# A four-layer graph network on one core: border steps of the message loop redrawn, and its variance moved to VectorE between two normalising passes

## The reference

```
def layer2(h, adj, W1, b1, g1, be1, W2, b2, g2, be2):
    m_j = einsum('bnd,do->bno', h, W1[:D])
    m_i = einsum('bnd,do->bno', h, W1[D:])
    pre = m_j[:, None, :, :] + m_i[:, :, None, :] + b1      # every pair i, j
    msg = gelu(layernorm(pre) * g1 + be1)                   # exact gelu
    agg = einsum('bijo,bij->bio', msg, adj)
    return layernorm(concatenate([h, agg], -1) @ W2 + b2) * g2 + be2
```

## Time and profile before

| | |
|---|---|
| median of three runs | 4009.07 us |
| profiled execution | 4007.12 us, of which its span 4005.3 us |
| DVE busy | 3267.3 us (82%) |
| PE busy | 3231.7 us (81%), mean granted clock 0.913 |
| ACT busy | 2663.1 us (66%) |
| POOL busy | 1939.6 us (48%) |
| transfers | 41 GB/s read and written over the span |

### The profile page before, as it was taken

How to read it: one execution, slowest core, us unless ns; L and a number is a source line. 1 busy time by engine, 2 the same in 40 slices (tenths; PEclk the granted TensorE clock), 3 DMA queues, 4 the chain that set the end, 5 groups by cost and what they waited for, 6 DMA issues and landing times.

```text
span 4005.3 us, 92223 instructions
## 1 busy us (share of the span) xinstructions
PE 3231.7 (81%) x24743; PEld 2745.1 (69%) x24840; DVE 3267.3 (82%) x11961; ACT 2663.1 (66%) x6659; POOL 1939.6 (48%) x1598
## 2 busy tenths in 40 slices
PE   3484688787888889788788888888897887888888
PEld 2273667677676777767677776767777676776777
DVE  4788888888888888888888888888888888887830
ACT  2484776848667585766848676685857668495753
POOL 1182753719355382744718273461827447182730
PEclk7596889999899999989999998999999899999999
DMA  2010102012020210202011020202102020110200
GB/s 82 29 53 29 50 9 75 24 36 73 5 79 16 67 37 30 72 3 80 24 51 48 30 68 2 83 22 62 37 30 72 4 80 24 41 46 9 61 8 21
DMA packets 147064, 167.74 MB, mean 42 GB/s; under 512 B 13232, under 2 KB 100912, under 8 KB 146736
## 3 DMA queue, kind: packets, MB, share of 16 engines
q1 hardware_dynamic: 146736, 163.96, 13.5%
HBM read 151.33 MB, written 12.58 MB: 41 GB/s over the span
## 4 chain that ended last, share of the span: by engine, by line
issue 27%; PE 20%; POOL 19%; DVE 19%; ACT 9%; DVEq 3%; POOLq 1%; ACTq 0%; DMA 0%; SPq 0%
POOL v_z L570 13%; PE n_bank_c L1604 4%; PE n_bank_d L1621 3%; PE n_bank_d L1622 3%; POOL v_prstd L581 2%; PE n_bank_d L1618 2%; DVE v_top_at L1077 2%; POOL v_pvar L578 2%; PE n_bank_b L1679 2%; ACT v_rows L813 1%; DVE v_top L1074 1%; DVE v_normed L1168 1%; ACT v_pair L878 1%; DVE v_adj_x L1082 1%; PE n_bank_b L1835 1%
## 5 line engine op out<-in xcount | busy, mean ns | idle before, releaser
L570 POOL TENSOR_TENSOR v_z<-v_z,all_bc_L_gnn_be 128x512 f32<-128x512 f32 x620 | 787.1, 1271 | 50.5 <-DVE v_z L1128 24.2
L781 ACT ACTIVATE v_diag<-all_ident,v_value 128x128 f32<-128x128 f32 x2480 | 754.0, 386 | 0.0
L1522 PE MATMUL n_bank_d<-v_diag,v_msg 128*128 128x128 f32 x4960 | 637.8, 283 | 31.0 <-ACT v_diag L781 29.9
L1522 PEld LDWEIGHTS n_bank_d<-v_diag,v_msg 128*128 128x128 f32 x4960 | 594.3, 196 | 36.7 <-ACT v_diag L781 32.9
L581 POOL TENSOR_TENSOR v_prstd<-v_pvar,all_neg_half 128x8 f32<-128x8 f32 x310 | 578.9, 1868 | 25.8
L1513 PE MATMUL n_bank_b<-v_parts,v_onehot 128*128 128x128 f16 x5472 | 379.9, 227 | 181.1 <-ACT n_bank_b L730 180.9
L1513 PEld LDWEIGHTS n_bank_b<-v_parts,v_onehot 128*128 128x128 f16 x5472 | 327.4, 101 | 236.1 <-ACT n_bank_b L730 231.2
L1604 PE MATMUL n_bank_c<-all_l_wsd,v_fT 128*128 128x256 f32 x1792 | 449.6, 393 | 29.3 <-ACT v_adjT L715 26.8
L1513 PE MATMUL n_bank_c<-v_parts,v_onehot 128*128 128x128 f16 x4960 | 339.2, 224 | 131.8 <-ACT n_bank_c L730 131.1
L725 ACT ACTIVATE v_fT<-n_bank_d,all_l_c 128x256 f32<-128x256 f32 x256 | 119.9, 474 | 462.3 <-PE n_bank_d L1622 462.1
L1128 DVE SCALAR_TENSOR_TENSOR v_z<-n_bank_c,v_prstd,all_bc_L_gnn_g 128x128 f32<-128x128 f32 x1240 | 345.3, 342 | 89.5 <-POOL v_prstd L581 89.4
(11 more groups left out here) (277 smaller groups left out, 6617.3 us busy)
## 6 DMA issues: line engine op xcount, KB each, us to landing
v_spread<-slot_rows SPq DMA_DIRECT2D x342, 256.0 KB, 3.2
v_adj_l<-in_adj SPq DMA_DIRECT2D x128, 256.0 KB, 4.0
v_adj_x<-in_adj SPq DMA_DIRECT2D x64, 256.0 KB, 3.7
v_ring<-in_x SPq DMA_DIRECT2D x16, 512.0 KB, 5.6
out_x<-v_xout SPq DMA_DIRECT2D x64, 128.0 KB, 1.9
slot_rows<-v_indexT SPq DMA_DIRECT2D x16, 256.0 KB, 2.0
w_wu<-in_L_gnn_wu SPq DMA_DIRECT2D x4, 192.0 KB, 2.5
all_W<-in_L_gnn_W SPq DMA_DIRECT2D x2, 128.0 KB, 4.0
```

What stands on the lines that cost most here:

```text
L570: nc.gpsimd.tensor_tensor(z[par][:, units], z[par][:, units], wide(bc["L2_gnn_be1"])[:, units], ALU.add).then_inc(sem["z_ready"], 1)
L781: ins = nc.scalar.activation(diag[par][:, u], ident[:], ACT.Copy, scale=value[:, u, bass.ds(slot, 1)])
L1522: ins = nc.tensor.matmul(ps_agg[:, u // NB, (u % NB) * P:(u % NB + 1) * P], msg[par][:, u], diag[par][:, u], start=False, stop=False, skip ...
```

## The change

**Variance.** `pvar` leaves POOL and is made by DVE, by the same operation on the same buffers. In a step it stands between the second and the third instruction of the second half of the normalising, and waits for the statistics of the slot. POOL's `prstd` still waits for it.

**Borders.** The last two steps of a group are written out behind the loop (their count is `body*2 + 2`): they make no one-hot matrices, and the very last one no seeding and no gathering. Spreads, one-hot matrices and gatherings are now as many as slots, and the extra wait of DVE at the end is gone. The number of slots is kept two smaller in `n_slots` (one small instruction and a drain more), with the same number of steps for the groups here. ACT's last diagonals stand before the gelu of the first half of the last slot and not behind it.

**Taking slots.** All 8 units are taken in one round, so there are half as many rounds of twice the size; `ratios` stands after the first round and `clip` behind the last one. The number of rounds is `((n+1)//2*2 + 9)//8` with the smaller n: for 22 slots it is 3 where it was 4, for 18 and 20 slots it stays 3.

```diff
@@ pool slots @@
                     if not first:
                         shift(1 - par, step, 0)
-                    pool.wait_ge(sem["stats_done"], step * 2 + 2)
-                    pool.sem_inc(keep["held"], 1)
-                    nc.gpsimd.tensor_scalar(pvar[:].rearrange("p (q u) -> p q u", u=2), pstats[:, par, :, :, 2], 1.0 / D,
-                                            UP * UP * LN_EPS, ALU.mult, ALU.add).then_inc(sem["pvar_ready"], 1)
                     pool.wait_ge(sem["pvar_ready"], step + 1)
@@ dve slots @@
+                def variances(par, step):
+                    dve.wait_ge(sem["stats_done"], step * 2 + 2)
+                    v.tensor_scalar(pvar[:].rearrange("p (q u) -> p q u", u=2), pstats[:, par, :, :, 2], 1.0 / D,
+                                    UP * UP * LN_EPS, ALU.mult, ALU.add).then_inc(sem["pvar_ready"], 1)
+
-                def normalise(par, half_):
+                def normalise(par, half_, between=None):
                     for u in range(half_ * HALF, (half_ + 1) * HALF):
+                        if between and u == half_ * HALF + 2:
+                            between()
                         ins = v.scalar_tensor_tensor(z[par][:, u], ps_m[par][:, u], prstd[:, par, u:u + 1],
...
-                    if not first:
+                    if first:
+                        variances(par, step)
+                    else:
                         dve.wait_ge(sem["msg_ready"], step * 2 + 2)
-                        normalise(1 - par, 1)
-                    pick(dve.snap(step + g * 2 + 2), par)
+                        normalise(1 - par, 1, between=lambda: variances(par, step))
+                    if not last:
+                        pick(dve.snap(step + 2), par)
...
-                dve.reg_add(count, count, pairs * 2)
+                dve.reg_add(count, count, body * 2)
+                ending = dve.snap(count)
+                for par in range(2):
+                    dve_step(par, dve.snap(ending + par), last=True)
+                dve.reg_add(count, count, 2)
                 after = dve.snap(count)
-                dve.wait_ge(sem["gathered"], (after + g) * 2 + 2)
@@ act slots @@
-                def act_step(par, step, slot, second=False):
+                def act_step(par, step, slot, second=False, last=False):
-                    act.wait_ge(sem["z_made"], step * 2 + 1)
-                    seed(1 - par, 0)
+                    if not last:
+                        act.wait_ge(sem["z_made"], step * 2 + 1)
+                        seed(1 - par, 0)
...
                 gelu(0, act.snap(after - 1), 1)
+                diagonals(1, after, act.snap(body * 2 + 1))
                 gelu(1, after, 0)
-                diagonals(1, after, act.snap(pairs * 2 - 1))
                 gelu(1, after, 1)
@@ pe slots @@
+                    if not last:
+                        pe.wait_ge(sem["onehot_ready"], step + 2)
+                        gather(1 - par, pe.snap(step + 1), 0)
+                        gather(1 - par, pe.snap(step + 1), 1)
@@ dve keep_slots, mix @@
-                v.tensor_scalar(n_slots[0:1, bass.ds(a, 1)], needed_g[:], 7.0, float(N), ALU.max, ALU.min)
+                v.tensor_scalar(needed_g[:], needed_g[:], float(N), -2.0, ALU.min, ALU.add)
+                dve.drain()
+                v.tensor_scalar(n_slots[0:1, bass.ds(a, 1)], needed_g[:], 7.0, None, ALU.max)
...
-                    take_slots(a, 0)
-                    ratios()
-                    take_slots(a, 1, between=clip)
+                    take_slots(a, between=ratios)
                     dve.drain().then_inc(sem["index_ready"], 1)
+                    clip()
```

More of the change, by code:

```diff
@@ L461, in slots @@
             def slots(a):
[L462 to L464 removed]
+                body = sp.snap(n_body)
+                before = sp.snap(count)
+                with sp.Fori(2, body + 1) as i:
                     for par in range(2):
@@ L1067, in take_slots @@
                     dve.wait_ge(adjx_in[b], a * 16 + 16)
                 dve.sem_inc(keep["held"], 1)
-                n = dve.value_load(n_slots[0:1, bass.ds(a, 1)], min_val=7, max_val=N)
-                full = dve.snap(((n + 1) // 2 * 2 + 10) // 8 - 1)
+                n = dve.value_load(n_slots[0:1, bass.ds(a, 1)], min_val=7, max_val=N - 2)
+                full = dve.snap(((n + 1) // 2 * 2 + 9) // 8 - 1)
                 def eight(r, more):
-                    for u in units:
+                    for u in range(UNITS):
@@ L1524, in aggregate, with pe_step @@
                     ins.then_inc(sem["summed"], 1)
-                first_ahead = pe.snap(before + g * 2)
-                pe.wait_ge(sem["onehot_ready"], first_ahead + 1)
+                pe.wait_ge(sem["onehot_ready"], before + 1)
                 for half_ in range(2):
                     pe.wait_ge(sem["parts_ready"], g * GB + 2 * half_ + 2)
-                    gather(0, pe.snap(before + g), half_)
-                def pe_step(par, step, slot, first=False, second=False):
-                    ahead = pe.snap(step + g * 2 + 2)
-                    pe.wait_ge(sem["onehot_ready"], ahead)
-                    gather(1 - par, pe.snap(step + g + 1), 0)
-                    gather(1 - par, pe.snap(step + g + 1), 1)
+                    gather(0, before, half_)
+                def pe_step(par, step, first=False, second=False, last=False):
+                    if not last:
+                        pe.wait_ge(sem["onehot_ready"], step + 2)
+                        gather(1 - par, pe.snap(step + 1), 0)
+                        gather(1 - par, pe.snap(step + 1), 1)
                     if not (first or second):
@@ L1539, in pe_step @@
                             aggregate(par, pe.snap(step - 1), half_)
-                pe_step(0, before, 0, first=True)
-                pe_step(1, pe.snap(before + 1), 1, second=True)
-                with pe.Fori(1, pairs) as i:
+                pe_step(0, before, first=True)
+                pe_step(1, pe.snap(before + 1), second=True)
+                with pe.Fori(1, body) as i:
                     for par in range(2):
-                        slot = pe.snap(i * 2 + par)
-                        pe_step(par, pe.snap(before + slot), slot)
-                pe.reg_add(count, count, pairs * 2)
+                        pe_step(par, pe.snap(before + (i * 2 + par)))
+                pe.reg_add(count, count, body * 2)
+                ending = pe.snap(count)
+                for par in range(2):
+                    pe_step(par, pe.snap(ending + par), last=par == 1)
+                pe.reg_add(count, count, 2)
                 after = pe.snap(count)
```

85 lines of the change are left out of this document (41 added, 44 removed).

## The result

The changed kernel takes 3896.29 us (median of 4 runs, 3888.37 to 3898.42) against 4010.61 us before (the three runs given above and one more): ratio 0.9712, interval 0.9694 to 0.9731. I had said 3893. The profiled execution spans 3892.5 us instead of 4005.3, 112.8 less, against 115.0 forecast.

The account below looks back on a forecast made before the run. Bound: a POOL and DVE ring of 4.85 us a step, four engines above 80%. Savings 101.4 + 3.2 + 3.7 + 6.7 = 115.0 us gave 3892.1 profiled, 3894 on the runs' scale, stated as 3893; range 3863 to 3942.

Parts of the forecast that it names:

- The ring of the earlier trace: Pair loop before the change: POOL's power, shifts and pvar with DVE's normalising close a ring of 4.85 us a step.
- `pvar` off POOL: Pair loop, POOL: without the variance instruction ahead of the power, the ring loses 0.29 us a step.
- the wait joined to the normalising: Pair loop, DVE: the wait for prstd stands on the normalising itself, not a register instruction ahead, saving 0.09 us a step.
- The variance's wait: Pair loop, DVE: the variance is held until POOL's shift ends, a wait of 0.26 us, taken as upper bound.
- The power at 1.64: Pair loop, POOL: the power starts free of one-hot work and takes 1.64 us, bounds 1.64 and 1.88.
- The step: Pair loop: distance between powers falls from 4.85 to 4.50 us; loops save 4.4 + 97.0 = 101.4 us.
- the highest floor: Pair loop: the largest of the floors given by the rings of the new step, put at 4.44 to 4.56 us.
- The way around: Pair loop: seeding, gathering, statistics and normalising across engines take 8.95 us for two steps, a floor of 4.48.
- Starts and ends: The 16 groups' borders: about 0.2 us saved at each start, 3.2, and 0.23 at each end, 3.7.
- The round that disappears: Stage ahead of the 22 slots: falls from 153.3 to a usual 146.6 us, 6.7 saved, once.
- Mix at 0: Stages between loops: ratios waits 5 to 6 us, offset by clip, copies and drains; net -0.6 to +2 each, taken as 0.
- The case that I called likeliest: Whole kernel: step 4.44 to 4.56 us and mix near nothing, giving 3865 to 3925 us; chance 0.72.

Follow-up runs that it names:

- a2: The changed kernel with the variance put back on POOL, leaving only the border edits and new order of mix: 3950.45 us, ratio 0.9854.
- c2: The changed kernel with the variance back on POOL and DVE's wait for prstd on its own instruction ahead of the normalising: 3983.54 us, ratio 0.9934.
- a1: The kernel before with only the variance moved from POOL to DVE; loop, borders and mix order unchanged: 3917.32 us, ratio 0.9774.
- b1: The changed kernel with the variance one instruction later, between third and fourth pass of the second normalisation: 3899.05 us, ratio 0.9730.
- b2: The changed kernel with the variance one instruction earlier, between first and second pass of the second normalisation: 3947.88 us, ratio 0.9857.
- c3: The changed kernel with the first of a step's two one-hot instructions moved directly behind the variance: 3946.44 us, ratio 0.9842.
- b3: The changed kernel with two pairs of ACT's eight diagonals made by one copy each, two units getting their neighbour's slot values: 3866.49 us, ratio 0.9656.
- b4: The changed kernel with two pairs of ACT's diagonals made by one copy each and the variance one instruction later: 3866.94 us, ratio 0.9651.
- a4: The changed kernel with the order of mix as before, slots taken in two halves of four units: 3908.63 us, ratio 0.9750.
- a3: The changed kernel with the four subtractions of ratios moved behind the looped rounds, ahead of the last one: 3891.28 us, ratio 0.9706.
- c1: The changed kernel with ratios behind the looped rounds and PE making layer 0's sums and outputs earlier: 3930.91 us, ratio 0.9807.
- d1: The changed kernel with ratios behind the looped rounds, layer 0's sums and the supports earlier on PE, logarithms earlier on ACT: 3964.19 us, ratio 0.9894.

## Why the prediction was right

- **The ring of the earlier trace rows** was read rightly. `pvar` off POOL and the wait joined to the normalising are separate terms, 0.29 and 0.09 by my sum; a2 and c2 show the second as 0.10 and 0.12. In the new step the second is worth nothing, because POOL's ring no longer holds it: a1, where the wait still stands on its own, has 4.424 as well.
- **The variance's wait** was right in kind, and its bound of 0.26 too high: 0.19 of DVE's queue (283 ns, ending 0.03 behind the shift). b1 and b2 show that it is the shift's end.
- **The power at 1.64** was right (1647 ns), and so was its reason (c3).
- **The step** I put at 4.50; it is 4.425. The term that was mis-sized is the highest floor. For DVE I had 4.46 and b3 shows 4.38. For ACT I had 4.44 to 4.53 and it is 4.42: the lower end was the true one, since where ACT has no idle time each operation starts before the last one ends. The way around, 4.48 by my sum, lies above the step that came out. Most of its excess is the variance's wait, which I had at 0.26 and which is 0.19: with it the two steps come to 8.88, 4.44 each. My 4.44 to 4.56 for the highest floor did not follow from the list either, whose highest were 4.48 to 4.53. At 4.425 my sum reads 17 x 0.335 + 277 x 0.425 = 123 instead of 101.4 (294 x 4.425 is 124.6 under the old loops); the loops are 106 shorter.
- **The 18 us between** lie at the loops' starts: the loops take 1319.3, while 294 x 4.425 = 1301.0. I had no term for them. 15.9 are in the third and fourth distance of a loop, and 10 of the 16 loops have a distance above 5 there. The windows between powers 3, 4 and 5 of a loop, in a group that has it and in one that has not:

```profile
1808.93:1814.12 5.19, 5.18 (x40) 5.18 (x41) 4.47 (x16) 4.99 (x13) 4.16 (x3) 0.50 0.24 54
1814.12:1819.61 5.49, 5.49 (x71) 5.48 (x70) 4.46 (x16) 4.70 (x12) 4.16 (x3) 0.95 0.13 48
2041.51:2045.88 4.37, 3.97 (x48) 3.62 (x48) 4.37 (x16) 4.37 (x12) 4.15 (x4) 1.00 0.17 63
2045.88:2050.36 4.48, 3.95 (x48) 3.61 (x48) 4.47 (x16) 4.48 (x14) 4.17 (x4) 1.00 0.17 59
```

At granted clock 0.50 PE is busy throughout and sets the step, 5.2 instead of 4.4. In the next one, 5.5, the clock is back at 0.95 and PE is still busy throughout, with 71 matmul records instead of 48: it works off what was left, as I read it. At 1.00 it has 0.4 of air. Before, the clock at a loop's start was low too, in most loops less so, and the step had the air for it (distances 2 and 3 of a loop, windows of the kernel before):

```profile
1864.13:1869.00 4.87, 3.39 (x38) 2.90 (x37) 4.35 (x15) 4.53 (x12) 4.59 (x5) 0.73 0.43 134
1869.00:1873.87 4.87, 4.44 (x36) 4.27 (x34) 4.29 (x15) 4.53 (x13) 4.61 (x5) 0.65 0.20 57
```

In two of its 16 loops the clock fell to 0.50 for two distances, and the one behind took 5.33 and 5.35 there too. What sets where the clock falls the runs do not show.

- **Starts and ends** (3.2 and 3.7): the last power of a loop is 1.65 instead of 1.87, yet the stages other than that of 22 slots lose only 1.6 in sum, so most of this was not seen. They follow the granted clock. Usual stages, one each at 0.92 and 0.93, of the changed kernel and of the borders alone:

```profile
2107.86:2254.43 146.57, 127.53 (x697) 103.85 (x695) 123.66 (x481) 85.56 (x205) 38.65 (x26) 0.92 0.09 29
```

```profile
2145.13:2290.03 144.90, 124.94 (x686) 101.93 (x690) 123.12 (x478) 85.17 (x204) 38.81 (x27) 0.93 0.09 30
```

DVE's busy time differs by 0.5; PE is 2.6 us busier in the one that is 1.7 longer, though with 697 matmul records against 686 not all of that need be the clock. Stages of ratios later go from 144.4 at 0.93 to 148.3 at 0.91. Between borders alone and the changed kernel the stages grow by 21.9; the 13 full ones go from 145.1 at a mean clock of 0.924 to 146.7 at 0.915. So part of what the loops gain is given back at a lower clock. That the faster loop is what lowers it would be the obvious reading, and the other runs speak against it. The loops of c3 take 1377.1, near the 1395.8 of the borders alone, and its stages 2175.6; those of b4 take 1305.4, less than in the changed kernel, and its stages 2166.1. The two kernels with stages of 2155 (a2, c2) are those with the new borders and the variance on POOL. Every kernel with the variance on DVE has 2166 or more; why their stages run at a lower clock stays open.
- **The round that disappears**: 5.5 instead of 6.7.
- **Mix at 0**: `ratios` waits 3.5 where I said 5 to 6, and the whole reorder gains about 11 by a4. That cover was the danger I named ("if it is more"): there is cover, but it is DVE's and ACT's next waits, not PE's layer 3 alone (a3, c1, d1). `clip` behind all rounds costs ACT a wait in the stages that lack a layer: 12.3 in each of the first two, without layer 3, and 3.6 in the last, without layer 0, of 28 in all.

The forecast of 3893 came out within 4 us by luck: against it, the step saved 23 us more, the loop starts cost 18 that I had no term for, and the rest of the program saved 7 less. The case that I called likeliest is the one that happened, with its cause and its time; its step lies 0.015 under the 4.44 where I had begun the range.

## What to carry to other kernels

Price an instruction that moves to another engine three times: what it takes there, what it waits for there, and what it no longer hides. Then list every floor of the new step; when the step falls by 9%, the next floors (here ACT's 4.42 and DVE's 4.38) decide, whatever the old ring would still allow (here 4.25, an estimate), and an engine without idle time runs nearer to its starts' spacing than to its durations. Read a step from several in a row: a median over steps that alternate is none of them. A saved wait in a stage of in-order queues is worth only what the next wait behind it leaves, and that is measured, not summed.
